# Weight splits of an attention kernel at other places: GpSimd's subtractions behind given VectorE copies, half of the roundings on ScalarE

## The reference

```python
x = x + attn(layernorm(x), Wq, bq, Wk, bk, Wv, bv)
x = x + ffn(layernorm(x), weight, scale_weight, bias)
# attn, 16 heads of 64:
q, k, v = (split_heads(h @ W + b) for W, b in ...)
ctx = local_attention(q, k, v)        # block of 128 queries sees 256 keys around it
idx = [0] + top_62_of(norm(q)) + [t - 1]            # 64 global queries per head
ctx[idx] = softmax(q[idx] @ k.T / 8) @ v            # these see all keys
# ffn: h @ (weight * scale_weight[:, None]).T + bias
```

## Time and profile before

| what | value |
|---|---|
| median of three runs | 2069.39 us |
| the profiled execution, own time | 2069.18 us |
| its span | 2067.6 us |
| TensorE busy | 1989.8 us, 96% |
| VectorE busy | 1538.0 us, 74% |
| ScalarE busy | 1003.6 us, 49% |
| GpSimd busy | 602.8 us, 29% |
| mean granted TensorE clock | 0.989 |

### The profile page before, as it was taken

The page is one execution under the profiler, slowest core; times in us unless marked ns, Lnnn a source line. Parts: engine busy times, 40 slices in busy tenths (PEclk is TensorE's granted clock), DMA queues, the critical chain, the costliest instruction groups (busy, mean ns, idle before and its releaser), DMA issues.

```text
span 2067.6 us, 36786 instructions
## 1 busy us (share of the span) xinstructions
PE 1989.8 (96%) x11264; PEld 1657.4 (80%) x11264; DVE 1538.0 (74%) x2917; ACT 1003.6 (49%) x1435; POOL 602.8 (29%) x478
## 2 busy tenths in 40 slices
PE   6998998999999999999889999999999999999999
PEld 6876887878878878788678887888888878888887
DVE  5597887774888777749887787488777876666664
ACT  4325765773257657732567677325766761000000
POOL 2333223124342231243412412424223203121211
PEclk9999999999999999999999999999999999999999
DMA  3437667754377677543666776427778654333331
GB/s 123 148 108 149 145 149 154 134 115 128 114 160 151 147 163 135 117 129 113 154 142 137 159 152 115 113 81 153 153 148 194 128 115 168 141 132 135 138 122 71
DMA packets 533830, 280.79 MB, mean 136 GB/s; under 512 B 433264, under 2 KB 498870, under 8 KB 533680
## 3 DMA queue, kind: packets, MB, share of 16 engines
q1 hardware_dynamic: 505584, 186.76, 41.8%
q0 software_dynamic: 23776, 76.63, 11.9%
q10 hardware_dynamic: 4320, 15.73, 1.9%
HBM read 122.73 MB, written 51.44 MB: 84 GB/s over the span
## 4 chain that ended last, share of the span: by engine, by line
PE 68%; DVE 15%; issue 7%; DMA 5%; ACT 3%; SPq 1%; DVEq 1%; POOL 0%; ACTq 0%; POOLq 0%
PE proj L649 33%; PE proj L810 16%; PE pv L768 7%; DMA p_turned<-p_parts 5%; PE pv L790 3%; DVE p_parts L1524 3%; DVE x_norm L1482 2%; PE turn L756 2%; DVE top_idx L1480 2%; PE score L756 2%; DVE top_val L1478 2%; PE turn L799 1%; PE score L782 1%; DVE q_sq L1444 1%; PE proj L924 1%
## 5 line engine op out<-in xcount | busy, mean ns | idle before, releaser
L649 PE MATMUL proj<-xT_hi,w_hi 128*128 128x512 f32 x1536 | 411.2, 410 | 13.6 <-ACT xT_hi L1037 9.8
L649 PE MATMUL proj<-xT_hi,w_lo 128*128 128x512 f32 x1536 | 419.2, 402 | 0.0
L649 PE MATMUL proj<-xT_lo,w_hi 128*128 128x512 f32 x1536 | 382.0, 391 | 0.0
L456 POOL CAST w_hi<-w_raw 128x1024 fp32r<-128x1024 f32 x96 | 108.5, 1130 | 917.8 <-PE proj L649 713.8
L1524 DVE COPY p_parts<-probs 128x1024 uint16<-128x1024 uint16 x320 | 270.0, 863 | 112.7 <-DMA p_turned<-p_parts 54.0
L1140 ACT COPY pT<-p_turned 128x1024 uint16<-128x1024 uint16 x256 | 332.8, 1369 | 20.8 <-DMA p_turned<-p_parts 20.4
L649 PEld LDWEIGHTS proj<-xT_lo,w_hi 128*128 128x128 f32 x1536 | 288.6, 188 | 63.8
L649 PEld LDWEIGHTS proj<-xT_hi,w_hi 128*128 128x128 f32 x1536 | 280.1, 192 | 72.7 <-issue 13.6
L649 PEld LDWEIGHTS proj<-xT_hi,w_lo 128*128 128x128 f32 x1536 | 283.0, 191 | 59.4
L768 PEld LDWEIGHTS pv<-v_nat,pT 128*128 128x128 f32 x2048 | 248.6, 193 | 37.6 <-issue 21.1
L768 PE MATMUL pv<-v_nat,pT 128*128 128x65 f32 x2048 | 246.9, 274 | 19.7 <-DVE ctx_out L1560 14.8
(11 more groups left out here) (179 smaller groups left out, 3011.8 us busy)
## 6 DMA issues: line engine op xcount, KB each, us to landing
w_raw<-in_wstream POOLq DMA_DIRECT2D x94, 512.0 KB
x_buf<-in_rows SPq DMA_DIRECT2D x41, 512.0 KB, 3.8
q_rows<-pT SPq DMA_DIRECT2D x64, 256.0 KB
ctx_rows<-ctx_out SPq DMA_DIRECT2D x128, 128.0 KB, 2.9
out<-q_store ACTq DMA_DIRECT2D x30, 512.0 KB, 2.6
q_store<-in_cols POOLq DMA_DIRECT2D x28, 512.0 KB, 5.3
q_store<-ctx_rows SPq DMA_DIRECT2D x28, 512.0 KB, 4.1
x_buf<-in_rows POOLq DMA_DIRECT2D x14, 512.0 KB, 5.1
```

The lines of the kernel that those rows point to most:

```text
L456: pool.tensor_copy(w_hi[b][:, :], w_raw[b][:, :]).then_inc(w_hi_set, 1)
L649: mm = pe.matmul(proj[:, bank, :], w[b][:, k * P:k * P + P], x[:, k, half * HALF:half * HALF + HALF], start=(m == 0), stop=(m == 23), skip ...
```

## The change

Four things are changed.

1. GpSimd, pairs: in the loop over `hp` = 0 to 5, which splits the slices of pair `hp + 2`, GpSimd no longer rounds. `split_low` waits for a place of VectorE's stream, then for `w_high` (ScalarE's rounding), and only subtracts. The place for v is `parted_p(n, hp, 2)`, behind both copies of step 2 of pair `hp`; for k it is `parted_v(n, hp + 1, 2)`, behind the last v copy, which VectorE makes early in pair `hp + 1`. The splits of the next batch's slices 0 and 1 to 4 wait in the same way, for `parted_v(n, 7, 1)` (in pair 6) and `parted_v(n, 7, 2)` (in pair 7), and still round on GpSimd. The column and row loads between them move by one split. The slices of the query stage and of the pairs 0 and 1 are split as before.
2. ScalarE: `weight_hi` rounds a whole slice, for v ahead of place 2 and for k at the pair's end, in the pairs 0 to 5: 12 a batch, 48 in all.
3. ScalarE, columns: two of eight first-half columns are rounded at (6, 2), four at (6, 3), and two at (6, 4), where there were four and four at (6, 3) and (6, 4); and place 4 stands ahead of `join_p(n, hp, STEPS - 1)`.
4. VectorE: `split_q` of pair 0 stands behind the norms of pair 1, at the start of the query stage.

```diff
         LO_AT = {(6, 3): (0, 1), (6, 4): (2, 3), (7, 0): (4, 5, 6, 7), (7, 1): (0, 1, 2, 3), (7, 2): (4, 5, 6, 7)}
-        HI_AT = {(6, 3): (0, 1, 2, 3), (6, 4): (4, 5, 6, 7), (7, 0): (0, 1, 2, 3), (7, 1): (4, 5, 6, 7)}
+        HI_AT = {(6, 2): (0, 1), (6, 3): (2, 3, 4, 5), (6, 4): (6, 7), (7, 0): (0, 1, 2, 3), (7, 1): (4, 5, 6, 7)}
...
+            def parted_p(n, hp, s):
+                pool.wait_ge(p_parted, 2 * (n * (PAIRS * EVENTS) + hp * EVENTS + s) + 4)
+
+            def parted_v(n, hp, k):
+                pool.wait_ge(v_parted, n * (PAIRS * V_PIECES) + hp * V_PIECES + k + V_PIECES + 1)
...
+            def split_low(n, what, j, load=True):
+
+                i, b = PAIRS + 2 * j + (what == "k"), int(what == "k")
+                pool.wait_ge(w_high[b], n * (PAIRS - 2) + j - 1)
+                apart(pool)
+                pool.tensor_tensor(w_lo[b][:, :], w_raw[b][:, :], w_hi[b][:, :].bitcast(F32),
+                                   ALU.subtract).then_inc(w_split[b], 1)
+                if load:
+                    load_slice(n, i, n * BUFS + PAIRS // 2 + j)
...
                 for what in "vk":
                     split_pair(n, what, 0)
+                load_column(n, 0)
                 if following:
-                    load_rows(n, 2)
+                    for b in range(2):
+                        load_row(n, 2, b)
                 split_pair(n, "v", 1)
                 store_rows(n, 0)
-                load_column(n, 0)
                 load_columns(n, 0)
                 split_pair(n, "k", 1)
                 gather(n, 0)
                 for hp in range(PAIRS - 2):
                     j = hp + 2
-                    split_pair(n, "v", j, load=following or j < PAIRS - 1)
+                    parted_p(n, hp, 2)
+                    split_low(n, "v", j, load=following or j < PAIRS - 1)
+                    if hp > 0:
+                        load_column(n, hp)
+                    if hp == 0 and following:
+                        load_row(n, 3, 0)
                     if hp == HALF_PAIRS - 1:
                         store_rows(n, 1)
+                        load_columns(n, 1)
+                        gather(n, 1)
+                    parted_v(n, hp + 1, 2)
+                    split_low(n, "k", j, load=following or j < PAIRS - 1)
                     if hp == 0 and following:
-                        load_rows(n, 3)
+                        load_row(n, 3, 1)
                     if hp == 1:
                         load_last_column(n, following)
-                    split_pair(n, "k", j, load=following or j < PAIRS - 1)
-                    if hp == HALF_PAIRS - 1:
-                        load_columns(n, 1)
-                        gather(n, 1)
-                    load_column(n, hp + 1)
+                load_column(n, PAIRS - 2)
                 if following:
-                    for i in range(4):
+                    parted_v(n, PAIRS - 1, 1)
+                    split_next(n, 0)
+                    parted_v(n, PAIRS - 1, 2)
+                    for i in range(1, 5):
                         split_next(n, i)
-                    split_next(n, 4)
                     scatter(n)
...
+            def weight_hi(n, what, j):
+
+                b = int(what == "k")
+                act.wait_ge(raw_in[b], 16 * (n * BUFS + PAIRS // 2 + j))
+                apart(act)
+                act.copy(w_hi[b][:, :], w_raw[b][:, :]).then_inc(w_high[b], 1)
...
                     for k in range(1, V_PIECES):
                         join_v(n, hp, k)
+                if not (early or last):
+                    weight_hi(n, "v", hp + 2)
                 if last:
                     out("k", 0, 1)
                 columns(2)
...
                 global_exps(u)
+                columns(4)
                 join_p(n, hp, STEPS - 1)
-                columns(4)
                 if early and not following:
                     ahead_hi(0)
                 out("k", 1, 3)
+                if not (early or last):
+                    weight_hi(n, "k", hp + 2)
...
                 for hp in range(1, PAIRS // 2):
                     norms_of(n, hp)
+                    if hp == 1:
+                        split_q(n * PAIRS, 0)
...
                 part_v(n, 0, 1)
-                split_q(n * PAIRS, 0)
                 top_find(n, 1, 0)
```

More of the change, by code:

```diff
@@ L145, in build @@
         w_hi_set = sem("w_hi_set")
+        w_high = [sem(f"w_high{b}") for b in range(2)]
         w_split = [sem(f"w_split{b}") for b in range(2)]
@@ L466, in load_slice, with load_row @@
                 pool.dma_start(w_raw[b][:, :], wstream[(i + 2) % SLICES]).then_inc(raw_in[b], 16)
-            def load_rows(n, j):
-                for b in range(2):
-                    pool.wait_ge(rows_seen, n * TILES + 2 * j + b - 1)
-                    apart(pool)
-                    pool.dma_start(x_buf[:, b, :], rows_in[n * TILES + 2 * j + b + TILES]).then_inc(last_rows_loaded[b], 16)
+            def load_row(n, j, b):
+                pool.wait_ge(rows_seen, n * TILES + 2 * j + b - 1)
+                apart(pool)
+                pool.dma_start(x_buf[:, b, :], rows_in[n * TILES + 2 * j + b + TILES]).then_inc(last_rows_loaded[b], 16)
             def load_column(n, k):
```

4 lines of the change are left out of this document (3 added, 1 removed).

## The result

The changed kernel takes 2043.46 us (median of 4 runs, 2040.40 to 2047.63); runs of the kernel before beside it have a median of 2068.36. The ratio is 0.9887, 95% interval 0.9847 to 0.9926: faster by 1.1%. The profiled execution took 2047.63 us, 21.6 less than that of before.

What follows compares the result with a forecast made beforehand. TensorE was taken to bound the kernel, busy 1989.8 of 2067.6 us. Terms of -5.9, -15.3, -4.0, -6.9 and -1.0 sum to -33.1, taking 2069.2 to 2036 us, range 2020 to 2052.

Steps and rivals of the forecast that it cites:

- blocked copies: VectorE's copies of probabilities near a pair's start, held by GpSimd's subtraction: 4.20 us for two, median of one 0.694.
- First query split: Ahead of a batch's first scores: moving the split removes TensorE's waits for `qT_lo`, -5.9 us in four batches.
- Pairs 1 and 2: Of 17.3 us excess, k's subtraction behind the last v copy removes all but 2: -15.3 us.
- ScalarE's roundings: 48 roundings of 1.1 us fit ScalarE's idle time ahead of steps 0 and 3: price 0; GpSimd's relief gains nothing.
- Pairs 4 and 5: Excess of 13.6 us from blocked copies goes, new meetings cost 1.6 us in each of six pairs: -4.0 us.
- Pair 7: Batches 0 to 2: earlier casts save 13.5 us of TensorE's waiting, new waits cost 6.6: -6.9 us.
- Batch 3: At its end, the wait for `ahead_lo` shortens as two casts leave the way of ScalarE's rounding: -1.0 us.
- signs that I had named: Right: no `p_parts` copy over 1.5 us in pairs 1 to 6, `qT_lo` wait gone, column instructions up to 3.6 us.
- the change does not do what it says: Rival, 0.08: waits for `v_parted` met at once, or blocked copies not the cause of long stretches; 2056 us.
- The new meetings strike in every pair: Rival, 0.12: v's subtraction blocks `qT_hi` by 1.2 us in 18 further pairs too; 2059 us.

Runs made afterwards that it cites:

- f3: As f1, but with the first query split and the load of column 0 both at their old places; 2033.98 us, ratio 0.9800.
- f2: As f1, but with the 48 roundings back on GpSimd as before the change; 2075.63 us, ratio 0.9994.
- f1: Changed kernel without GpSimd's waits for places in pairs 1 to 6, keeping those for the next batch's slices in pair 7; 2026.04 us, ratio 0.9767.
- g1: Kernel before with one part alone: ScalarE rounds the 48 slices and GpSimd only subtracts; 2058.91 us, ratio 0.9899.
- e4: Changed kernel with the 48 roundings back on GpSimd ahead of each subtraction, places kept; 2065.13 us, ratio 0.9959.
- e2: Changed kernel with the first query split back at its old place, the load of column 0 left early; 2058.89 us, ratio 0.9924.
- e3: Changed kernel with the old column table and the last step's joins ahead of the columns again; 2045.95 us, ratio 0.9864.
- e1: Changed kernel without any of GpSimd's waits for places; 2043.59 us, ratio 0.9864.

## Why the prediction was right, and where not

The time was forecast within 7.5 us (2036 against 2043.5) and the direction with it; of the 33 us forecast 25 came. The blocked copies were rightly seen as the largest loss. But the sum came out in part by luck: a step priced at nothing does by itself what the forecast asked of the places, and the places in the pairs 4 to 6 cost more than they give once it is there.

- **First query split, -5.9.** Right in its wait: `qT_lo` is gone, and the norm copy is next late, but not with nothing: 1.8 us in three. Clean, the split's place is worth 6 to 8 us (f3). Pair 0 did not follow: it is 1.6 us longer in four, by copies of step 0 that GpSimd's split of k's slice holds.
- **Pairs 1 and 2, -15.3.** Measured -9.7. The reading of the blocked copies stands (f2 brings them back, f1 and g1 do without). The cure that I named, k's place, works (e4 against f2), but it is not needed: with ScalarE's rounding and without any place the excess of pairs 1 to 3 is 0.6. The remaining 7.6 in the changed kernel are mostly one late transposition, for which I had left 2: VectorE idles 6.88 us in pair 1 of batch 2. It is not chance. That pair takes 42.7, 42.7, 39.5 and 39.0 us in the four traces with k's place (changed, e2, e3, e4) and 37.1 in e1 and f1. The place holds back GpSimd's loads behind k's subtraction as well: in the changed kernel they are issued 12.4 and 14.4 us into the pair, just ahead of the transposition, which lands 9.5 us after its issue; in f1 they are issued at 5.5 and 7.5. That the loads delay it is argued from these times, not tested. One reading was loose: not one copy took about 3.02 us, but four did, one each in four of the long pairs.
- **ScalarE's roundings: price 0, "GpSimd loses 48 x 1.1 us of rounding from a stream that idles: nothing".** The step that failed. The price was right: ScalarE's rounding took 1.03 to 1.10 us, and in f1 pairs with both roundings take 37.1. The gain was not nothing: 2.3% between f1 and f2 and 1.0% alone (g1). In the changed kernel itself, with its places, it is about 20 us (e4), for the most part in pair 6, whose weights come in time. I counted the rounding by GpSimd's idle time. What counts is when the visit begins and when it ends. Before, it mostly began 0.2 us into a pair, as soon as TensorE left the buffer, with 3.5 us to go, and where both copies of the global step ran into it the pair was long; ScalarE comes to its rounding only behind its own work for the copies, so GpSimd is released 2.2 to 3.9 us into the pair (pair 4 apart), mostly in the gap between the copies of the global step and those of step 0. That a later start is enough is shown in the pairs 1 to 3 by e4; whether the shorter visit alone would be, no run shows.
- **Pairs 4 and 5, -4.0.** Measured -4.7, with the meetings about as priced: 0.6 to 2.5 us in six pairs. But they were a loss to be avoided, not a price for the gain: pair 5 without place has no excess. In pair 4 the first of them is the gather, which now stands ahead of k's subtraction and puts it onto a copy of step 1.
- **Pair 7, -6.9.** Measured, with the query stage and so with three of the query splits: -15.4. `xT_hi` waits are gone; the new waits are 0.8 a batch instead of 2.2. Of it the places are 9.7 (e1 against f1), the columns' order 4 (e3), the query split 3.4 (f3 against f1); they add up to more than the whole, within the noise of single traces.
- **Batch 3, -1.0.** From its pair 7 to the end 2.0 came. Pair 6, which I left at nothing, lost 6.9. There the place puts k's subtraction directly onto VectorE's row roots, and two bias additions that wait for it run behind it (the two engines; `ln_bits` is 128 x 2 elements):

```profile
1600.72 3.16 POOL L521 TENSOR_TENSOR w_lo<-w_raw,w_hi 128x1024 fp32r<-128x1024 f32 x1 [16.86 <-DVE q_sq L1550]
...
1601.87 2.03 DVE L1396 TENSOR_SCALAR ln_minus_half<-ln_mv 128x2 f32<-128x2 f32 x1
...
1604.00 5.15 DVE L1398 TENSOR_SCALAR ln_bits<-ln_var 128x2 uint32<-128x2 uint32 x1
...
1604.38 2.41 POOL L585 TENSOR_TENSOR w_raw<-x_buf,bias_b 128x1024 f32<-128x1024 f32 x1
...
1606.74 2.38 POOL L585 TENSOR_TENSOR w_raw<-x_norm,bias_b 128x1024 f32<-128x1024 f32 x1
...
1615.11 1.30 PE L793 MATMUL pv<-v_nat,pT 128*128 128x65 f32 x5 [3.82 <-ACT v_nat L1129]
```

The signs that I had named read as follows: copies of up to 2.14 us in pair 4, none elsewhere in pairs 1 to 6; column instructions up to 3.15 us. They all came, and none of them could tell the places from the rounding. Only undoing each did. Of the rivals, "the change does not do what it says" is true of v, whose place is always passed. "The new meetings strike in every pair" is true of the meeting and not of its cost: v's subtraction stretches `qT_hi` from 0.68 us to between 1.75 and 2.06 in 14 of 32 pairs, about as priced. In f1 it does so in 17, and most of these take 37.1 us.

```profile
L1488 DVE TENSOR_SCALAR qT_hi<-q_store x32: 682/1748/2033, 61.6 to 1609.8; 128x1024 fp32r<-128x1024 f32 x32
```

## What to carry to other kernels

When a change both shortens an engine's visit and tells it where to go, test the two apart: here each of them cured the blocked copies, and with the shorter visit in place the waits only held it back onto other work. Ask of work on a side engine when it starts and ends, relative to the copies that it can block and to those who want its result; its share of idle time does not say. And when an edit is undone to measure it, look for what else was put behind its signal in an in-order stream.

## What the runs showed of the hardware

- An instruction of VectorE on 128 x 2 elements, usually 0.16 us, took 5.15 us, across two GpSimd additions that the trace shows without a gap (1604.38 to 1609.12); it ended with the second.
- `qT_lo`, of which no row before showed a meeting, took up to 3.30 us after the change (median 1.23), in 2 of 32 (the line's group: count, duration ns min/median/max). This is what the Trainium skill ("SBUF — State Buffer", Who interferes with whom) states for an instruction with two SBUF inputs beside one of GpSimd that reads SBUF, and here a trace now agrees:

```profile
L1492 DVE SCALAR_TENSOR_TENSOR qT_lo<-q_store,qT_hi x32: 1224/1226/3304, 62.4 to 1626.2; 128x1024 fp32r<-128x1024 f32 x32
```

- A stall can cost more than itself. Ten-microsecond windows of the changed kernel behind the 3.82 us wait and around a smaller one (columns as in the stretches above; the clock is the third from the end):

```profile
1600.00:1610.00 10.00, 10.00 (x69) 8.12 (x68) 9.86 (x9) 0.65 (x1) 8.39 (x4) 1.00 0.77 154
1610.00:1620.00 10.00, 6.18 (x26) 5.36 (x25) 7.39 (x23) 8.83 (x14) 0.00 (x0) 0.71 0.32 60
1640.00:1650.00 10.00, 9.21 (x46) 7.87 (x47) 8.20 (x16) 5.21 (x9) 0.00 (x0) 0.83 0.25 51
```

The granted clock is 0.71 and 0.83 in the mean of these windows, so TensorE had its lower level (1.2 GHz) for part of them. Of the 7.7 us of excess in that pair 3.8 are the wait, the only one of TensorE in it.
- Issuing a transposing DMA takes SP 1.24 us in the median and up to 5.51 us in some executions. The three pairs with an issue of 4.97 to 5.51 took 42.4 to 44.7 us, one with 4.77 took 38.9. What brings it about was not found.
